# A graph layer and mixture of experts on one core: the one-hots of four message blocks by one compare of two streams

## The reference, cut to what matters

```python
def _spmm_plus_eye(rows, cols, vals, X):
    msgs = vals[:, None] * X[cols]
    agg = jax.ops.segment_sum(msgs, rows, num_segments=N)
    return agg + X
...
support = feature @ W1
out = _spmm_plus_eye(rows, cols, vals, support)
out = _batchnorm_relu(out, gamma, beta)
out = _spmm_plus_eye(rows, cols, vals, out @ W2)
...
x = x + gnn(layernorm(x), src, dst, edge_weight)
x = x + moe(layernorm(x))
```

## Time and profile before

| | us |
|---|---|
| median of 3 runs | 4614.71 |
| lowest, highest | 4610.76, 4619.99 |
| the profiled execution | 4628.39 |
| its span, first to last instruction | 4626.6 |
| second stage in it, from 1225 to 1980 us | 755 |
| VectorE busy in the whole span | 3301.2 (71%) |
| GpSimd busy in the whole span | 2841.5 (61%) |

### The profile page before, as it was taken

The page is one execution under the profiler, slowest core; times in us unless marked ns, Lnnn a source line. Parts: engine busy times, 40 slices in busy tenths (PEclk is TensorE's granted clock), DMA queues, the critical chain, the costliest instruction groups (busy, mean ns, idle before and its releaser), DMA issues.

```text
span 4626.6 us, 83922 instructions
## 1 busy us (share of the span) xinstructions
PE 3828.6 (83%) x26914; PEld 3346.5 (72%) x26914; DVE 3301.2 (71%) x8596; ACT 2957.3 (64%) x6463; POOL 2841.5 (61%) x2961
## 2 busy tenths in 40 slices
PE   1688888888789998965688888888888888888888
PEld 1688788778677777744577777777777777777778
DVE  8788888888688888855466666666666666666656
ACT  3688888889777777753455555555555555555555
POOL 0477777767566565646666666666666666666551
PEclk9999999999899999976798998988998989999989
DMA  8788888888799898963333333333333333333221
GB/s 237 278 315 309 310 316 308 304 316 293 272 308 305 296 315 292 311 189 116 93 98 101 107 100 98 106 98 99 108 101 102 106 100 108 102 102 106 79 82 30
DMA packets 308791, 857.91 MB, mean 185 GB/s; under 512 B 47937, under 2 KB 133018, under 8 KB 305852
## 3 DMA queue, kind: packets, MB, share of 16 engines
q0 software_dynamic: 140032, 442.58, 29.1%
q1 hardware_dynamic: 166148, 396.53, 26.8%
q10 hardware_dynamic: 2172, 13.35, 0.8%
HBM read 545.71 MB, written 306.56 MB: 184 GB/s over the span
## 4 chain that ended last, share of the span: by engine, by line
PE 54%; DVE 16%; issue 12%; ACT 8%; another core or an unknown queue 4%; DMA 4%; POOL 2%; SPq 0%; ACTq 0%; DVEq 0%; POOLq 0%
PE ps L1765 11%; PE ps L1744 10%; PE ps L1635 4%; PE ps L1464 3%; PE ps L893 2%; DVE S L1410 2%; PE ps L1639 2%; PE ps L1637 2%; PE ps L894 2%; PE ps L862 2%; DMA L<-msgd 2%; PE ps L851 2%; ACT A L959 2%; DVE low L1414 2%
## 5 line engine op out<-in xcount | busy, mean ns | idle before, releaser
L1550 POOL DMA_INDIRECT G<-h,tabT x1440 | 1461.7, 1015 | 828.8 <-issue 383.3
L1843 ACT ACTIVATE ps<-ps,b1T 128x500 f32<-128x500 f32 (+1 forms) x432 | 266.8, 618 | 780.4 <-remote 462.9
L959 ACT ACTIVATE A<-ps,A 128x256 f32<-128x256 f32 x1728 | 689.4, 510 | 83.1 <-PE ps L894 78.7
L1010 POOL DMA_INDIRECT msgd<-A,tabT x432 | 551.5, 1277 | 285.9 <-ACT A L959 169.8
L1616 ACT ACTIVATE gH<-G,tabT 128x256 fp32r<-128x256 f32 x960 | 449.0, 500 | 186.8 <-remote 64.1
L1994 DVE SCALAR_TENSOR_TENSOR X<-ps,X 125x256 f32<-125x256 f32 x800 | 347.0, 477 | 283.2 <-remote 239.5
L893 PE MATMUL ps<-winH,DT 128*128 128x256 f32 x1728 | 474.2, 306 | 51.8 <-issue 18.5
L1596 DVE SCALAR_TENSOR_TENSOR gL<-G,tabT,gH 128x256 fp32r<-128x256 f32 x960 | 442.3, 479 | 80.7 <-ACT gH L1616 52.8
L894 PE MATMUL ps<-winL,DT 128*128 128x256 f32 x1728 | 437.3, 285 | 0.0
L1637 PE MATMUL ps<-gH,s 128*125 128x256 f32 x1067 | 349.8, 329 | 63.1 <-issue 30.6
L893 PEld LDWEIGHTS ps<-winH,DT 128*128 128x128 f32 x1728 | 333.8, 193 | 60.6 <-issue 37.7
(11 more groups left out here) (333 smaller groups left out, 11094.8 us busy)
## 6 DMA issues: line engine op xcount, KB each, us to landing
L<-msgd SPq DMA_DIRECT2D x400, 520.0 KB, 5.6
A<-sbd SPq DMA_DIRECT2D x54, 861.0 KB
msgd<-A SPq DMA_DIRECT2D x100, 325.0 KB
G<-h,tabT POOLq DMA_INDIRECT x1440
winR<-h SPq DMA_DIRECT2D x108, 128.0 KB
A<-in_x SPq DMA_DIRECT2D x10, 1120.0 KB
h<-A ACTq DMA_DIRECT2D x10, 1120.0 KB
acc<-h SPq DMA_DIRECT2D x10, 1120.0 KB
```

The costliest lines, as they stand in the source:

```text
L959: e.activation(M[:, n, 0:F], psum[4 + v % 4][:, (n % 2) * F:(n % 2 + 1) * F], ACT.Identity, scale=M[:, n, F + 2:F + 3]).then_inc(evc, 1)
L1010: e.indirect_dma_start(msgd, bass.IndirectOffsetOnAxis(ap=idxI[g % 4][:, t:t + 1], axis=0), msg[g % 3][:, t * 4 * RW:(t + 1) * 4 * RW], No ...
L1550: e.indirect_dma_start(B.G[c % GRL], None, of, bass.IndirectOffsetOnAxis(ap=tab3[:, m, 0:1].bitcast(I32), axis=0)).then_inc(gatl[c % GRL], 16)
```

## The change

In `dve_read` the four instructions that compare the gapped table with one scalar each become one TENSOR_TENSOR with two streams of 4 x 125 elements: `iota_f`, repeated for each of the four columns, and the destinations, each repeated 125 times. It writes the same four one-hots and raises the same semaphore. Nothing else is edited: `B.iota` is still built, and `tail_select` still uses it.

```diff
                 if u >= SRD:
                     e.wait_ge(r_mm, u - SRD + 1)
-                for k in range(n):
-                    m = e.tensor_scalar(S3[:, k, :].rearrange("p (a b) -> p a b", b=5), B.iota, L3[:, k, F + 1:F + 2], None, ALU.is_equal)
-                m.then_inc(r_sel, 1)
+                e.tensor_tensor(S3, iota_f[:, 0:R].rearrange("p (o f) -> p o f", o=1).broadcast_to([P, n, R]),
+                                L3[:, :, F + 1:F + 2].broadcast_to([P, n, R]), ALU.is_equal).then_inc(r_sel, 1)
                 e.wait_ge(r_hi, split_upto(u, whole))
```

## The result

| | before | after |
|---|---|---|
| median of 20 runs | 4613.03 | 4622.03 |
| ratio, 95% interval | | 1.0021 (1.0011 to 1.0031) |
| the profiled execution's span | 4626.6 | 4617.8 |
| second stage in it | 763.2 | 759.7 |

The kernel became **slower by 9 us, 0.2%**. The forecast was 4607, faster by 8. The profiled executions stand the other way round: single executions scatter, over 25 us in the 20 runs of before and over 33 us in those of after, and before's profiled one, with 4628.39 us, took 15 us more than its median. The profile can show where VectorE's time went, but only many runs show a total this small.

A forecast was written before the change was run, and what follows sets the result against it. VectorE was taken to set the second stage's pace until ScalarE's limit, 60 us away. The walk's -24, +5 for high parts and +10 for GpSimd's lateness gave -9, taken as -8: 4614.7 - 8 = 4607 us, range 4572 to 4655.

The forecast's parts named there:

- the walk: Four second-stage pieces stepped through with new durations: 0.09 us gained per piece, -24 us over 267; program range 4590 to 4624.
- The price at the port: VectorE and GpSimd taking turns at SBUF: 0.52 us at a boundary, 0.32 on average per GpSimd low part.
- The step that failed is the first: Second stage, between dense layers: VectorE sets the pace, so each microsecond saved there shortens the program until another engine is late.
- ScalarE's limit: Second stage: ScalarE's work lets no more than 75 us be gained, taken as 60 with waits for loads.
- it takes the low part the moment it is made: TensorE in the second stage: 79 waits for VectorE's low part, 21.4 us in sum, read as VectorE setting the pace.
- The term for high parts: First low part behind 13 of 25 dense layers waits for the high part anyway, losing the compare's saving: +5 us.
- whatever it does: At each second-stage dense layer VectorE waits some 4 us for ScalarE, however fast it is; 95.2 us in all.
- The term for GpSimd's lateness: Block ends: GpSimd's low part is late, TensorE needs it and VectorE waits for TensorE; 0.1 us per block, +10.
- the rival of the cheap port: Second stage: GpSimd's low parts fall mostly into gaps, 0.15 us or less each; some -55 us, 4560; chance 0.15.

The follow-up runs named there:

- cut pair: Kernel before and changed kernel, both ended behind the second stage with the third left out and rows stored: 2070.45 and 2074.45 us, +4.0.
- no_low0 pair: Kernel before and changed kernel, each without GpSimd's low part, TensorE's work kept the same: -19.6 and -44.2 us against the kernel before.
- all4 pair: Kernel before and changed kernel, each with VectorE making all four low parts and GpSimd only table copies: +22.2 and -36.4 us against the kernel before.
- after_no_low0: Changed kernel without GpSimd's low part, TensorE taking the second column's twice instead: -44.2 us against the kernel before, ratio 0.9892.
- after_col0_last: Changed kernel with TensorE taking the first column's low part, GpSimd's, last of four instead of first: +3.1 us against the kernel before, ratio 1.0000.
- four_two_stream: Kernel before with its four compares kept apart but each given two streams: 4310.86 us, +53.3 us against the kernel before, ratio 1.0129.
- before_all4: Kernel before with VectorE making all four low parts and GpSimd only the table copies: +22.2 us against the kernel before, ratio 1.0056.
- before_no_low0: Kernel before without GpSimd's low part, TensorE's work kept the same: -19.6 us against the kernel before, ratio 0.9948.
- after_again: Changed kernel as it is, timed again on an experiment chip: +3.6 us against the kernel before, ratio 1.0019.

## Why the prediction was wrong

The measured 4622 us lies in the range, and even in the walk's own of 4590 to 4624. The sign was wrong: 8 us faster was forecast, with 0.40 for faster against 0.30 for slower, and 9 us slower came.

**The price at the port: right.** The prediction said 0.52 us at a boundary, 0.32 on average for GpSimd's low part and 0.03 for each of 1.5 copies, 0.365 per piece in terms. Measured: 0.53 in the row of 1607.34. Against the undisturbed 0.67 and 0.95 us, the compare's mean of 905 ns and the low part's of 1086 are 0.371 more per piece, copies included; against the kernel without GpSimd's low part, 0.363, so that the low part alone cost somewhat more than 0.32 and the copies less than 0.045. The compare's 0.59 us and the walk's order of turns were right too. VectorE was to do 24 us less work in the net, and did 17 less.

**The step that failed is the first: "A microsecond saved on VectorE between the layers is thus a microsecond of the program, until another engine is late."** It took VectorE as the only pace-maker up to a limit, and ScalarE's limit as a wall far behind. In the cut pair VectorE's work fell by 15.6 us, its waiting rose by 21.8, and the stage became 6.2 us longer; in the profiles of the whole kernels it is 16.8, 13.3 and 3.5 shorter. Nor does it hold where GpSimd's low part is out of the way: 98 us less on VectorE bring 24.6 us of program (the no_low0 pair), 106 us less bring 59 (the all4 pair). Over the kernels in which GpSimd's low part doesn't meet a two-stream compare from SBUF, VectorE's busy time and the stage go 679 and 791, 621 and 752 to 763, 609 and 747, 573 and 733, 511 and 719 us: there is no wall but a slope, which gets flatter downwards (some 0.5 to 0.7 from 679 to 621, 0.23 from 573 to 511). These kernels differ in more than VectorE's work, so the slope is a description and no law. The faster VectorE is, the more pieces wait for the high part: 13 of them and 12 us before, 26 and 22 us after, 108 and 54 us in after_no_low0.

The rows had a sign of it. The prediction said of TensorE that "it takes the low part the moment it is made", from 79 waits; but there are 267 pieces in terms, and in most of them the profile has no such wait: something else was last.

**The term for high parts was too small.** I put +5 for compares whose saving is lost behind a dense layer. VectorE's waits for high parts rose by 10 us (12.6 in the cut pair), and those in the dense layers, which the prediction held fixed ("whatever it does"), by 2 (5.3 in the cut pair). Together that is 12 to 18 us, most or all of what VectorE saved. What made ScalarE's high parts come later against VectorE was not traced.

**The term for GpSimd's lateness had the wrong place.** I put +10 at the end of a block, where VectorE waits for TensorE. There it is 4.6 us, and it was 2.3 before. It shows as 25 us of TensorE's waiting for GpSimd's low part. Whether this reaches the program isn't shown: after_col0_last took the wait away without a gain beyond its interval. What is seen is that the kernels in which GpSimd meets the two-stream compare lie above others at the same busy time of VectorE: four_two_stream's stage 19 us over before_all4's, and the changed kernel's, at 604 and 758 to 762, above before_no_low0's 609 and 747.

**ScalarE's limit was too far off.** I took 60 us; with all of GpSimd's low parts gone the stage stands at 719, 33 to 44 us under before's 752 to 763, and the program 44 us under. So the rival of the cheap port, -55 us, was out of reach even with no low part to pay for. (The kernel has 27 dense layers, 23 for four blocks and 4 for two, where the prediction counts 25.)

Redone with what the runs showed, the sum is 16 to 17 us of work less on VectorE against 13 to 22 us more of waiting: about nothing or a small loss. What remains open is why the waits rose by just that much, and how the last few microseconds divide: the medians give +9.0 and +3.6, the cut pair +4.0, and the profiles' stages (-3.5 and +6.2) scatter as much as the effect.

## What to carry to other kernels

Before an instruction gets a second SBUF stream, look at what GpSimd does in SBUF at the same time: here VectorE's such instructions and GpSimd's took turns, and the saving was paid as waiting on both (0.53 us at a boundary). Where the helper's share is small, take it away rather than share: here 0.27 us more work per piece on VectorE was cheaper than 0.36 us of turns. And before a saving on a busy engine is counted in full, count how many of its instructions already wait now and then; here, with other engines nearly as busy, it was worth a half (59 of 106 us) or a quarter (24.6 of 98).

## What the runs showed of the hardware

- A compare whose table is a stream from PSUM left GpSimd free (668 ns, undisturbed, with a copy of 0.19 us inside it), while the same compare with both streams from SBUF had 905 ns beside GpSimd's low parts.
- When VectorE's two-stream instructions followed each other without a break, GpSimd's waiting low part ran at the next boundary (1607.42 to 1608.01), and the VectorE instruction behind it took 1.48 us instead of 0.95.
- A two-stream compare of 128x125 took 0.271 us at the least, the one-stream compare from the table with gaps 0.320. The gaps' form is the slower one by itself, and the better one only beside GpSimd.
- Where a kernel ran mattered more than the change: the kernel before took 4613 us in the 20 runs and 4252 to 4258 on the three chips of the experiments. The third stage makes most of the difference: it took 2637 us in the profile of before and 2297 in that of after_again, with a granted TensorE clock of 0.89 and 0.93 in it and 102 and 117 GB/s moved. What lies behind this isn't shown.
